# A four-layer graph network on one core: weights loaded later, and the first eight row blocks fed in two halves

## The chip, the cores and the metric

The kernel runs on one core of a Trainium2 chip. The metric is the device time of one execution in microseconds. The kernel before took 1255.84 us in the median of three runs (1253.23 to 1257.3).

## The reference

`x` is 4096 rows of 128 numbers, `adj` a sparse 4096 x 4096 matrix of which about one element in a thousand is not zero. Four layers follow one another; each takes the layer-normalised rows, clipped at zero, and adds its result to x:

```python
h = relu(layernorm(x)); x = x + L0(h, adj)   # relu((D^-1 A' h) W^T + b), A' = a*A + (1-a)*I
h = relu(layernorm(x)); x = x + L1(h, adj)   # two attention heads over the mask adj > 0
h = relu(layernorm(x)); x = x + L2(h, adj)   # one attention head over the mask, relu
h = relu(layernorm(x)); x = L3(h, adj)       # (A^T h) / column sums
```

All is float32. For this change only the start of layer 0 matters: the rows are normalised, multiplied by W (the kernel projects first and sums over neighbours afterwards), and the first products with tiles of `adj` begin.

## The kernel before

**Tiling.** The 4096 rows are 32 blocks of 128 (T = 32). Four groups of eight blocks (Q = 4 groups, S = 8) hold them: X in SBUF, the projected rows in G. The output is made in four quarters of 1024 rows. For a quarter q of a layer, TensorE runs through the 32 blocks k of the sum (`run`, L409): a tile of 128 x 1024 numbers of the transposed `adj` is the stationary operand in eight pieces, the 129 columns of G's block k stream, and the eight results are summed in PSUM (`acc`, L340). A float32 product shows as two MATMUL records, so a tile of eight products counts as 16; a float32 transpose is one record. Five such passes (`h` = 0 to 4) of four quarters make up the kernel.

**The start.** TensorE runs WARM = 38 transposes of the identity, then waits for W0 (`w0_loaded`). A group p is *fed* in four steps. VectorE takes bn_stats of its eight blocks in two halves and derives scale and shift (`statistics`, L847; `scales`, L867). ScalarE normalises X into V (L536). TensorE turns V into `turn` (eight transposes, L355); ScalarE copies `turn` to U in two copies of 512 columns (`widen`, L560); TensorE multiplies U with W0 into `mix` (L374); ScalarE copies `mix` into G in three copies (L612). For group 0 the normalising is divided: ScalarE does blocks 0 to 3 and signals `f_norm`, VectorE does blocks 4 to 7 (L1033 to L1037) and signals `rest_normal`. All eight are turned together, behind both signals.

**The order on each engine.** TensorE's order is written out by hand: `run` takes a dictionary of hooks, a hook of k is executed behind tile k. Each engine executes in its own order, and waits on semaphores. In quarter 0 of layer 0 the groups 1, 2 and 3 are turned and projected as hooks; tile 0, 8, 16 and 24 each wait for their group to be placed in G (`f_placed`). VectorE makes a mask of every tile (`masks`, L1042, one tensor_scalar of 128 x 1024 each) and has the statistics of groups 1 to 3 as hooks; group 1's begin behind mask 0 with a wait for `x_loaded[1]`, and its scale and shift are made behind mask 2.

**The queues.** SyncE issues, in this order: X's blocks 0 to 3 and 4 to 7 (group 0), W0, tiles 0 and 1, X's group 1, tiles 2 and 3, X's groups 2 and 3, then tiles 4 to 31. For quarter 0, eight slots hold tiles (FIRST = 8); tile 8 and later ones wait for their slot. GpSimd makes the identity and then issues 15 loads of weights (0.55 MB together: W2, both heads' projections, biases, gains, the diagonal; `loads`, L319 to L327). They are used by `scores_behind_projections` on TensorE (hook of tile 28), by `prepare` on VectorE behind mask 31, and by ScalarE ahead of quarter 1. GpSimd issues nothing after them.

Of the kernel before, what the change touches and what calls it, by code (L numbers as in the profile page):

```python
# [30 lines left out]
P = 128  # L31
# [33 lines left out]
def graph_layers(nc, x, adj, adj_t, diag, alpha, w0_t, bias0, ff0, ff0_t, ff1_t, attn, g1, b1, g2, b2,  # L65
                 w2, w2_t, a2, out, inputs1):
    N, D = x.shape
    T = N // P
    Q = 4
    S = T // Q  # L70
# [3 lines left out]
    HEADS = 2  # L74
    BANK = 512
    NB = (S + 2) // 3
    STREAM = 4
    FIRST = 8
    DEEP = 32
# [5 lines left out]
    with ExitStack() as ctx:  # L85
# [3 lines left out]
        def sem(name):  # L89
            return ctx.enter_context(nc.semaphore(name))  # L90
# [4 lines left out]
        G = sb("G", [P, 2, T, DW])  # L95
        ring = sb("ring", [P, 5, QC])
        U = sb("U", [P, S * DW])
        V = sb("V", [P, S, D])
        ident = sb("ident", [P, P])
# [20 lines left out]
        w0T = spare[:, 0:D]  # L120
# [22 lines left out]

        acc = ctx.enter_context(nc.psum_tensor("acc", [P, NB, BANK], F32))
        turn = ctx.enter_context(nc.psum_tensor("turn", [P, 2 * BANK], F32))
        mix = ctx.enter_context(nc.psum_tensor("mix", [P, NB, BANK], F32))
        mixed = mix[:, 0:2, :].rearrange("p b c -> p (b c)")
        mixed3 = mixed.rearrange("p (s d) -> p s d", d=D)
# [17 lines left out]
        x_first, rest_normal = sem("x_first"), sem("rest_normal")  # L166
        x_loaded = [sem(f"x_loaded{q}") for q in range(Q)]
# [8 lines left out]

        f_var, f_dev, f_scale, f_norm = sem("f_var"), sem("f_dev"), sem("f_scale"), sem("f_norm")
        f2_var, f2_dev, f2_scale, f2_in = sem("f2_var"), sem("f2_dev"), sem("f2_scale"), sem("f2_in")
        f_turned, f_wide, f_projected, f_placed = sem("f_turned"), sem("f_wide"), sem("f_projected"), sem("f_placed")

        top_placed, top_spread, bias_made, row_shifted = sem("top_placed"), sem("top_spread"), sem("bias_made"), sem("row_shifted")
# [4 lines left out]
        fall_made, fold_made, fixed_v, fixed_w = sem("fall_made"), sem("fold_made"), sem("fixed_v"), sem("fixed_w")  # L186
        acc_paused = [sem(f"acc_paused{b}") for b in range(NB - 1)]
        acc_scaled = sem("acc_scaled")
# [17 lines left out]
        def fixed(v):  # L206
            return isinstance(v, int)
# [105 lines left out]
        @block.gpsimd  # L313
        def _(pool):
            nc.gpsimd.memset(ident[:, :], 0.0).then_inc(ident_zero, 1)
            pool.wait_ge(ident_zero, 1)
            nc.gpsimd.affine_select(out=ident[:, :], in_=ident[:, :], compare_op=ALU.not_equal, fill=1.0,
                                    base=0, pattern=[[-1, P]], channel_multiplier=1).then_inc(consts_made, 1)
            loads = [(bias0_b, bias0.partition_broadcast(P)), (alphac, alpha.partition_broadcast(P)),  # L319
                     (w2raw, w2_t), (attnc[:, 0:4], attn), (attnc[:, 4:6], a2), (dsub[:, :], diag),  # L320
                     (proj1[:, 0:D], ff0_t[0]), (ff0T1, ff0_t[1])]
            loads += [(ff0raw[h], ff0[h]) for h in range(HEADS)]
            loads += [(c, v.rearrange("(c o) -> c o", o=1)) for c, v in ((g1c, g1), (b1c, b1), (g2c, g2), (b2c, b2))]
            loads += [(ff1T[:, :, :], ff1_t.rearrange("h c o -> c h o"))]
            assert len(loads) == WEIGHTS
            for dst, src in loads:
                pool.dma_start(dst, src).then_inc(weights_loaded, 16)  # L327

# [2 lines left out]
        def _(pe):  # L331
# [26 lines left out]
            def feed(p, weights, wide, spreads, posts):  # L358

                def turned():  # L360
                    pe.wait_ge(f_norm, p + 1)
                    if fixed(p) and p == 0:
                        pe.wait_ge(rest_normal, 1)
                    wait(pe, rows_kept, spreads)
                    turn_v().then_inc(f_turned, 1)

                def project():
                    pe.wait_ge(f_wide, p + 1)
                    if fixed(p) and p == 2 * Q:
                        pe.wait_ge(bias_made, late_top[2])  # L370
                    wait(pe, f_placed, p)
                    wait(pe, post_done, posts)
                    for s in range(S):
                        mm = pe.matmul(mix[:, s // 3, (s % 3) * PW:(s % 3) * PW + wide],  # L374
                                       U[:, s * P:(s + 1) * P], weights, start=True, stop=True,
                                       skip_group_check=True)
                    mm.then_inc(f_projected, 1)
                return turned, project
# [30 lines left out]
            def run(h, q, hooks):  # L409
                n = q + h * Q  # L410
                for k in range(T):
                    if h == 0:
                        pe.wait_ge(*loaded0(q, k))
                        if fixed(q) and q == 0 and k % S == 0:
                            pe.wait_ge(f_placed, k // S + 1)
                        lhs, used = tile0(q, k), slot_used
                    elif h == 4:
                        pe.wait_ge(deep_loaded[k % DEEP], (q * (T // DEEP) + k // DEEP + 1) * 16)
                        if fixed(q) and q == 0 and k % S == 0:
                            pe.wait_ge(f_norm, 4 * Q + k // S + 1)  # L420
                        lhs, used = stream3[:, k % DEEP, :], deep_used
                    else:
                        pe.wait_ge(e_made, (n - Q) * T + k + 1)
                        if fixed(q) and q == 0 and k % S == 0:
                            if h == 2:
                                pe.wait_ge(f_placed, 2 * Q + k // S + 1)
                            else:
                                pe.wait_ge(g_scaled[k // S], fixes[h])
                        lhs, used = E[k % EB], e_used
                        if k == 0 and h != 2 and not (fixed(q) and q == 0):  # L430
                            pe.wait_ge(fixed_v, fixes[h])
                    products(n, k, lhs, G[:, h % 2, k, :], used, fixes[h] if h in fixes and fixed(q) and q == 0 else 0)
                    if k in hooks:
                        hooks[k]()
# [4 lines left out]
                pe.transpose(one, ident[:, :], ident[:, :])  # L439
            pe.wait_ge(w0_loaded, 16)  # L440
            own = [feed(p, w0T, D, 0, 0) for p in range(Q)]
            own[0][0]()
            own[0][1]()

            def scores_behind_projections():
                pe.wait_ge(weights_loaded, 16 * WEIGHTS)
                pe.wait_ge(f_placed, Q)
                for h, raw in enumerate(ff0raw + [w2raw]):
                    mm = pe.matmul(one[:, 2 * h:2 * h + 2], raw, attnc[:, 2 * h:2 * h + 2], start=True, stop=True,
                                   skip_group_check=True)  # L450
                mm.then_inc(qv_summed, 1)
            run(0, 0, {2: own[1][0], 4: own[1][1], 10: own[2][0], 13: own[2][1], 18: own[3][0], 21: own[3][1],
                       28: scores_behind_projections})

            def stage0(q, more={}):
# [69 lines left out]
        def _(act):  # L525
# [8 lines left out]
            def normalise(dst, src, mul, add, func, done, n=S):  # L534
                for s in range(n):
                    ins = act.activation(dst(s), src(s), func, bias=add(s), scale=mul(s))  # L536
                if done is not None:
                    ins.then_inc(done, 1)

            def local(t):  # L540
                return lambda s: t[:, s:s + 1]
# [8 lines left out]
            def widen(got, n, done, scale_=None, bias_=None, halves=None):  # L550
# [9 lines left out]
                        ins = act.copy(dst, src)  # L560
                ins.then_inc(done, 1)

            def feed(h, p, q, between=(), ahead=None):

                def of_x(s):
                    return blocks(X, q, 1, s)[:, 0, :]
                if h == 2:

                    act.wait_ge(rows_kept, 1)
                    def known(i):  # L570
                        return lambda s: blocks(norms[:, i, :], q, 1, s)
                    settle()
                    normalise(of_v, of_x, known(0), known(1), ACT.Relu, f2_in)
                    act.wait_ge(f2_in, q + Q + 1)
                    normalise(of_v, of_v, known(2), known(3), ACT.Identity, f_norm)
                else:
                    deviation(f_var, p - Q + 1 if h > 2 else p + 1, f_dev)
                    act.wait_ge(f_scale, p - Q + 1 if h > 2 else p + 1)
                    settle()
                    if h == 4:  # L580
                        normalise(lambda s: blocks(G[:, 0, :, :], q, 1, s)[:, 0, 0:D], of_x, local(scale), local(shift),
                                  ACT.Relu, f_norm)
                        return
                    normalise(of_v, of_x, local(scale), local(shift), ACT.Relu, f2_in if h == 1 else f_norm,
                              S // 2 if fixed(p) and p == 0 else S)
                    if h == 1:
                        deviation(f2_var, q + 1, f2_dev)
                        act.wait_ge(f2_scale, q + 1)
                        normalise(of_v, of_v, local(scale), local(shift), ACT.Identity, f_norm)
                if ahead is not None:  # L590
                    ahead()
                if h in (1, 2):
# [686 lines left out]
```

## Time and profile before

| | |
|---|---|
| median of three runs | 1255.84 us (1253.23 to 1257.3) |
| the profiled execution, its own time | 1257.09 us |
| its span, first to last instruction | 1255.3 us |
| TensorE busy | 1238.2 us, 99% |
| VectorE, ScalarE, GpSimd busy | 751.2 us (60%), 349.8 us (28%), 9.0 us (1%) |
| mean granted TensorE clock | 0.997 |

The profiled execution takes 1.8 us more than its span, and lies 1.25 us above the median. Busy times are measured from the first to the last instruction. TensorE's clock has two levels here, 1.00 (2.4 GHz) and 0.50 (1.2 GHz).

### The profile page before, as it was taken

To read this page: it belongs to the slowest core of one execution; us is meant where nothing else is said; L and a number is where in the kernel's file an instruction comes from. 1 tells how busy PE (TensorE), PEld (TensorE's weight loads), DVE (VectorE), ACT (ScalarE), POOL (GpSimd) and SP (SyncE) were. 2 spreads that over 40 slices of the span, in tenths; PEclk is the share of its full clock that TensorE was granted. 3 is DMA by queue.
4 is the path that set the end of the run, shared out by engine and by line. 5 is a ranking of instruction groups with operands and counts; after the bars stand their busy time and mean duration, and the time that the engine had idled before them with its cause. 6 is when DMAs were issued, how large, how long until landed. Compare 5 with 4: busy or idle time off the path is not lost.

```text
span 1255.3 us, 26479 instructions
## 1 busy us (share of the span) xinstructions
PE 1238.2 (99%) x10979; PEld 1233.2 (98%) x10979; DVE 751.2 (60%) x1342; ACT 349.8 (28%) x872; POOL 9.0 (1%) x21
## 2 busy tenths in 40 slices
PE   7999999999999999999999999999999999999998
PEld 6999999999999999999999999999999999999998
DVE  4437463678786868687979797879687850000001
ACT  3322222243744343531333234343222120000000
POOL 2000000000000000000000000000000000000000
PEclk8999999999999999999999999999999999999999
DMA  8788886830000000000000000000000059999820
GB/s 271 245 263 297 269 288 207 287 110 2 18 1 18 0 17 0 17 1 19 1 17 0 17 1 18 1 1 2 1 0 0 2 199 408 408 411 403 297 68 18
DMA packets 47249, 144.47 MB, mean 115 GB/s; under 512 B 4784, under 2 KB 13248, under 8 KB 47168
## 3 DMA queue, kind: packets, MB, share of 16 engines
q1 hardware_dynamic: 42976, 139.08, 31.1%
q10 hardware_dynamic: 3696, 3.67, 0.8%
q8 instruction: 61, 1.00, 0.3%
q0 software_dynamic: 496, 0.55, 0.2%
q14 instruction: 20, 0.16, 0.0%
HBM read 139.09 MB, written 4.19 MB: 114 GB/s over the span
## 4 chain that ended last, share of the span: by engine, by line
PE 92%; DVE 4%; DMA 2%; ACT 1%; issue 1%; SPq 0%; DVEq 0%; ACTq 0%
PE acc L340 86%; PE mix L374 2%; DVE ring L1010 2%; PE turn L355 2%; PE mix L391 1%; DMA X<-in_x 1%; PE turn L351 1%; ACT V L536 0%; DMA ring<-in_adj_t 0%; DVE stats L851 0%; DVE stats L855 0%; ACT U L536 0%; DVE U L1122 0%; DVE mask L1154 0%; DVE mask L1048 0%
## 5 line engine op out<-in xcount | busy, mean ns | idle before, releaser
L340 PE MATMUL acc<-G,ring 128*128 128x129 f32 x6656 | 758.1, 275 | 2.3 <-DVE ring L1010 1.7
L340 PEld LDWEIGHTS acc<-G,ring 128*128 128x128 f32 x6656 | 750.2, 192 | 5.6 <-DVE ring L1010 3.9
L1010 DVE SCALAR_TENSOR_TENSOR ring<-ring,score,mask 128x1024 f32<-128x1024 f32 x384 | 483.7, 1281 | 136.7 <-PE acc L340 130.6
L340 PE MATMUL acc<-G,mask 128*128 128x129 f32 x3584 | 404.3, 276 | 1.3 <-ACT G L612 1.3
L340 PEld LDWEIGHTS acc<-G,mask 128*128 128x128 f32 x3584 | 403.2, 193 | 1.5 <-issue 1.5
L712 ACT COPY U<-acc 128x387 f32<-128x387 f32 (+1 forms) x60 | 25.5, 459 | 270.6 <-PE acc L340 269.3
L1048 DVE TENSOR_SCALAR mask<-mask 128x1024 f32 (+1 forms) x96 | 64.5, 691 | 58.2 <-DMA mask<-in_adj_t 57.5
L1224 DVE TENSOR_SCALAR zero<-U 128x8 f32<-128x8 f32 x3 | 0.5, 171 | 153.4 <-ACT U L712 153.4
L548 ACT ACTIVATE dev<-var 128x8 f32<-128x8 f32 x28 | 5.9, 210 | 250.7 <-DVE var L864 250.7
L677 ACT COPY ring<-turn 128x512 f32<-128x512 f32 x14 | 8.2, 586 | 121.5 <-DVE ring L1010 114.1
L1048 DVE TENSOR_SCALAR mask<-ring 128x1024 uint8<-128x1024 f32 x32 | 21.9, 693 | 31.4 <-DMA ring<-in_adj_t 21.5
L558 ACT ACTIVATE U<-turn,cols 128x512 f32<-128x512 f32 x32 | 23.2, 774 | 49.4 <-PE turn L355 49.4
L536 ACT ACTIVATE V<-X,shift,scale 128x128 f32<-128x128 f32 (+1 forms) x92 | 36.7, 481 | 0.0
L532 ACT ACT_TABLE_LOAD x26 | 33.4, 1283 | 1.2 <-PEq L1258 0.8
L374 PE MATMUL mix<-ring,U 128*128 128x128 f32 (+2 forms) x256 | 31.4, 276 | 1.2 <-ACT U L560 1.2
L355 PE MATMUL turn<-ident,V 128*128 128x128 f32 x192 | 25.9, 279 | 6.3 <-ACT V L536 4.6
L528 ACT COPY cols<-ident 128x1 f32<-128x1 f32 x44 | 8.6, 195 | 82.4 <-DVE shift L874 34.5
L374 PEld LDWEIGHTS mix<-ring,U 128*128 128x128 f32 x256 | 29.9, 191 | 1.4 <-ACT U L560 1.4
L1243 DVE SCALAR_TENSOR_TENSOR zero<-U 128x3 f32<-128x3 f32 (+1 forms) x3 | 0.5, 162 | 50.8 <-ACT U L712 50.8
L355 PEld LDWEIGHTS turn<-ident,V 128*128 128x128 f32 x192 | 22.3, 144 | 7.0 <-ACT V L536 5.0
L536 ACT ACTIVATE V<-U,shift,scale 128x128 f32<-128x128 f32 x64 | 25.5, 481 | 10.3 <-DVE shift L874 10.3
L612 ACT COPY G<-mix 128x384 f32<-128x384 f32 (+3 forms) x36 | 14.8, 461 | 42.2 <-PE mix L374 42.2
(139 smaller groups left out, 483.4 us busy)
## 6 DMA issues: line engine op xcount, KB each, us to landing
mask<-in_adj SPq DMA_DIRECT2D x128, 512.0 KB, 14.9
mask<-in_adj_t SPq DMA_DIRECT2D x96, 512.0 KB, 4.6
ring<-in_adj_t SPq DMA_DIRECT2D x32, 512.0 KB, 4.6
inputs<-V ACTq DMA_DIRECT2D x4, 512.0 KB, 2.6
V<-inputs SPq DMA_DIRECT2D x4, 512.0 KB, 3.9
X<-in_x SPq DMA_DIRECT2D x3, 512.0 KB, 12.8
out_x<-V ACTq DMA_DIRECT2D x3, 512.0 KB, 14.6
X<-in_x SPq DMA_DIRECT2D x2, 256.0 KB, 2.9
```

Of the source, the lines that this page charges most:

```text
L340: mm = pe.matmul(acc[:, b, (s % 3) * DW:(s % 3) * DW + DW], lhs[:, s * P:(s + 1) * P], g, start=(k == 0 and s % 3 == 0), stop=(k == T - 1) ...
L351: return pe.transpose(dst, col.broadcast_to([P, P]), ident[:, :])
L355: mm = pe.transpose(turn[:, s * P:(s + 1) * P], V[:, s, :], ident[:, :])
L374: mm = pe.matmul(mix[:, s // 3, (s % 3) * PW:(s % 3) * PW + wide], U[:, s * P:(s + 1) * P], weights, start=True, stop=True, skip_group_che ...
L391: mm = pe.matmul(mixed[:, s * P:(s + 1) * P], U[:, s * P:(s + 1) * P], ff1T[:, h, :], start=True, stop=True, skip_group_check=True)
L532: act.activation(warm[func], ident[:, 0:1], func)
L536: ins = act.activation(dst(s), src(s), func, bias=add(s), scale=mul(s))
L558: ins = act.activation(dst, src, ACT.Identity, bias=bias_, scale=scale_)
L612: ins = act.copy(blocks(G[:, h % 2, :, :], q, c, 3 * b)[:, :, 0:D], got[:, :, 0:D])
L712: act.copy(U[:, b * 3 * DW:b * 3 * DW + w], acc[:, b, 0:w]).then_inc(acc_taken, 1)
L1010: dve.scalar_tensor_tensor(E[k % EB], R, rank[h][:, k:k + 1], span(mask, (q * T + k) * QC, QC), ALU.max, ALU.mult).then_inc(e_made, 1)
L1048: dve.tensor_scalar(span(mask, (q * T + k) * QC, QC), tile0(q, k), 0.0, None, ALU.is_gt).then_inc(mask_made, 1)
```

## The change

GpSimd waits for X's group 1 (`x_loaded[1]`) before it issues its 15 loads. Group 0 is turned, widened, projected and placed in two halves of four blocks. The first half has signals of its own (`h_turned`, `h_wide`, `h_projected`, `h_placed`), the second takes those of the group. The first half is turned behind `f_norm`, the second behind `rest_normal`; W0 is still awaited ahead of both. Tile 0 waits for the first half, tile 4 for the second. ScalarE's part of it stands in a function of its own; it places each half with one copy of 4 x 128 columns from `mixed3`, a view of `mix` in which the eight blocks lie 128 columns apart. Group 1 is turned behind tile 4 instead of 2 and projected behind tile 6 instead of 4.

```diff
+    HALF = S // 2
@@ GpSimd
+            pool.wait_ge(x_loaded[1], 16)
             for dst, src in loads:
                 pool.dma_start(dst, src).then_inc(weights_loaded, 16)
@@ TensorE, turned() in feed
-                    if fixed(p) and p == 0:
-                        pe.wait_ge(rest_normal, 1)
@@ TensorE, run
-                        if fixed(q) and q == 0 and k % S == 0:
+                        if fixed(q) and q == 0 and k < S:
+                            if k % HALF == 0:
+                                pe.wait_ge(f_placed if k else h_placed, 1)
+                        elif fixed(q) and q == 0 and k % S == 0:
                             pe.wait_ge(f_placed, k // S + 1)
@@ TensorE, the start
-            own[0][0]()
-            own[0][1]()
+            for half in range(2):
+                pe.wait_ge(rest_normal if half else f_norm, 1)
+                for s in range(half * HALF, (half + 1) * HALF):
+                    mm = pe.transpose(turn[:, s * P:(s + 1) * P], V[:, s, :], ident[:, :])
+                mm.then_inc(f_turned if half else h_turned, 1)
+            for half in range(2):
+                pe.wait_ge(f_wide if half else h_wide, 1)
+                for s in range(half * HALF, (half + 1) * HALF):
+                    mm = pe.matmul(mixed[:, s * P:(s + 1) * P], U[:, s * P:(s + 1) * P], w0T,
+                                   start=True, stop=True, skip_group_check=True)
+                mm.then_inc(f_projected if half else h_projected, 1)
-            run(0, 0, {2: own[1][0], 4: own[1][1], 10: own[2][0], 13: own[2][1], 18: own[3][0], 21: own[3][1],
+            run(0, 0, {4: own[1][0], 6: own[1][1], 10: own[2][0], 13: own[2][1], 18: own[3][0], 21: own[3][1],
@@ ScalarE, instead of widen and the copies into G for group 0
+            def first_halves():
+                for half in range(2):
+                    act.wait_ge(f_turned if half else h_turned, 1)
+                    act.copy(U[:, half * BANK:(half + 1) * BANK], turn[:, half * BANK:(half + 1) * BANK]).then_inc(f_wide if half else h_wide, 1)
+                for half in range(2):
+                    act.wait_ge(f_projected if half else h_projected, 1)
+                    act.copy(G[:, 0, half * HALF:(half + 1) * HALF, 0:D], mixed3[:, half * HALF:(half + 1) * HALF, :])\
+                        .then_inc(f_placed if half else h_placed, 1)
```

## Rows read from the trace of the kernel before

**Rows 1.** The page: span; busy us, share of the span, instructions.

```profile
span 1255.3 us, 26479 instructions
PE 1238.2 (99%) x10979; PEld 1233.2 (98%) x10979; DVE 751.2 (60%) x1342; ACT 349.8 (28%) x872; POOL 9.0 (1%) x21
```

**Rows 2.** TensorE by stage: stretch, length, busy (instructions), granted clock, DMA share, GB/s.

```profile
21.30:24.96 3.66, 0.00 (x0) 0.83 1.00 366
24.96:30.70 5.74, 5.74 (x28) 0.51 0.97 388
...
82.70:1255.30 1172.60, 1164.89 (x10377) 1.00 0.29 105
```

**Rows 3.** TensorE's timeline, 0 to 45 us: start, length, count, idle before it.

```profile
10.08 1.09 PE L355 MATMUL turn<-ident,V 128*128 128x128 f32 x8 [1.71 <-DMA ring<-in_w_t]
12.33 2.05 PE L374 MATMUL mix<-ring,U 128*128 128x128 f32 x16 [1.16 <-ACT U L560]
15.70 5.60 PE L340 MATMUL acc<-G,mask 128*128 128x129 f32 x48 [1.32 <-ACT G L612]
24.96 1.97 PE L355 MATMUL turn<-ident,V 128*128 128x128 f32 x8 [3.66 <-ACT V L536]
26.72 5.58 PE L340 MATMUL acc<-G,mask 128*128 128x129 f32 x32
...
33.92 10.88 PE L340 MATMUL acc<-G,mask 128*128 128x129 f32 x96
44.64 1.04 PE L355 MATMUL turn<-ident,V 128*128 128x128 f32 x8
```

**Rows 4.** Timeline of all engines, 0 to 40 us.

```profile
1.69 0.67 POOL L327 DMA_DIRECT2D ring<-in_bias  x1 [0.21 <-issue]
...
7.15 1.64 ACT L536 ACTIVATE V<-X,shift,scale 128x128 f32<-128x128 f32 x4
...
8.25 0.43 DVE L1037 TENSOR_SCALAR V<-V 128x512 f32<-128x512 f32 x1
...
9.31 0.71 POOL L327 DMA_DIRECT2D ff1T<-in_ff_t  x1
...
11.21 1.07 ACT L560 COPY U<-turn 128x512 f32<-128x512 f32 x2 [2.41 <-PE turn L355]
...
14.42 1.14 ACT L612 COPY G<-mix 128x384 f32<-128x384 f32 x3 [2.14 <-PE mix L374]
...
17.50 0.87 DVE L851 BATCH_NORM_STATS2 stats<-X 128x6 f32<-128x128 f32 x4 [5.14 <-DMA X<-in_x]
...
21.72 3.18 ACT L536 ACTIVATE V<-X,shift,scale 128x128 f32<-128x128 f32 x8
```

**Rows 5.** SP's DMAs issued at 0.75, 1.80, 2.34, 3.29, 16.69: KB, us to landing.

```profile
X<-in_x SPq DMA_DIRECT2D x1, 256.0 KB, 2.8
...
ring<-in_w_t SPq DMA_DIRECT2D x1, 64.0 KB, 8.2
...
mask<-in_adj_t SPq DMA_DIRECT2D x1, 512.0 KB, 9.3
...
X<-in_x SPq DMA_DIRECT2D x1, 512.0 KB, 14.2
...
mask<-in_adj_t SPq DMA_DIRECT2D x1, 512.0 KB, 7.8
```

**Rows 6.** All engines (PE, PEld, DVE, ACT, POOL) by stage, then clock, DMA share, GB/s.

```profile
4.00:9.00 5.00, 4.37 (x28) 4.13 (x26) 4.11 (x21) 1.95 (x6) 5.00 (x10) 1.00 0.51 124
9.00:16.00 7.00, 3.44 (x27) 3.05 (x27) 0.69 (x1) 2.21 (x5) 1.02 (x2) 1.00 1.04 325
16.00:24.00 8.00, 5.30 (x48) 5.11 (x46) 4.56 (x20) 2.58 (x8) 0.00 (x0) 0.98 0.93 304
24.00:30.00 6.00, 5.04 (x24) 5.04 (x25) 4.38 (x14) 1.98 (x5) 0.00 (x0) 0.50 1.00 396
```

**Rows 7.** GpSimd's last load, issued at 9.31: KB, us to landing.

```profile
ff1T<-in_ff_t POOLq DMA_DIRECT2D x1, 128.0 KB, 7.1
```

More of the change, by code:

```diff
@@ L178, in graph_layers @@
         f2_var, f2_dev, f2_scale, f2_in = sem("f2_var"), sem("f2_dev"), sem("f2_scale"), sem("f2_in")
+        h_turned, h_wide, h_projected, h_placed = sem("h_turned"), sem("h_wide"), sem("h_projected"), sem("h_placed")
         f_turned, f_wide, f_projected, f_placed = sem("f_turned"), sem("f_wide"), sem("f_projected"), sem("f_placed")
@@ L589, in feed @@
                         normalise(of_v, of_v, local(scale), local(shift), ACT.Identity, f_norm)
+                if fixed(p) and p == 0:
+                    first_halves()
+                    return
                 if ahead is not None:
```

## The prediction

> **What bounds the kernel now.** I read the page first: TensorE is busy 1238.2 us of a span of 1255.3 [rows 1]. Only 17.1 us of the span are not matmul, and no other engine is near its limit. An edit to the start can therefore pay in two coins alone: idle time of TensorE, and time at the lower clock. The table by stage shows where they lie. From 82.70 us to the end TensorE is idle 7.7 us in 1172.6; at the start it is idle for a whole 3.66 us, and the 5.74 us behind that run at a granted clock of 0.51, that is at 1.2 instead of 2.4 GHz [rows 2]. TensorE's timeline then gives the order of the start [rows 3]: group 0's turn starts at 10.08, 1.71 us behind the warm-up, its projection at 12.33, the first sums at 15.70; after three tiles (48 matmuls, two for each product) TensorE waits until 24.96 for group 1. The brackets there name the releasers: W0's transfer for 1.71 us, ScalarE's normalised V for 3.66 us. The timelines of ScalarE and VectorE [rows 4] follow the second of these back: group 1's normalising starts at 21.72 and takes 3.18 us, its statistics start at 17.50, and they start there because X's second part lands there: it is issued at 3.29 and lands 14.2 us later [rows 5]. W0 is issued at 1.80 and lands 8.2 us later, at 10.0, though X's first 256 KB took 2.8 us [rows 5]. So both waits are DMA waits.
>
> Why is DMA late? From 4 to 9 us the engines move 124 GB/s at a busy share of 0.51, with four SP transfers outstanding; from 9 to 16 us they move 325, and 396 when tiles alone flow [rows 6]. The slow stretch is the one in which GpSimd issues its 15 loads (first at 1.69, last at 9.31) [rows 4]. That the loads cause it is an inference from the coincidence.
>
> **The change, part by part.** I compare with one common point: five tiles summed and group 1 turned. Before, that is at 26.72 + 5.58 = 32.3 us [rows 3].
>
> *Loads behind X's second part.* GpSimd has nothing behind the waiting loads. Their consumers (the scores behind tile 28, the constants on VectorE, ScalarE's second layer) come behind some 70 us; free. Without the loads, 1.64 MB are left to be moved at about 4.2 us (W0, tiles 0 and 1, X's second part). At 325 GB/s these take 5.0 us, so X's second part lands near 9.3 instead of 17.5, W0 near 4.5 (before, 10.0), tile 0 near 6 to 7 instead of 11.6 [rows 5, 6].
>
> *Halves.* W0 no longer holds anything: the turn now waits for the first normalising of V, done at 7.15 + 1.64 = 8.79; VectorE's half is done at 8.68 [rows 4]. TensorE turns from 8.84. One half turned is 1.09/2 = 0.55, to 9.4; ScalarE's copy of 512 columns is 1.07/2 = 0.53, to 9.95; the projection of eight blocks is 2.05 us, from 10.0 to 12.06; the second half's turn (to 9.95) and copy (to 10.5) lie beneath the first half's projection, and the placing of half one (about 0.55) beneath the second's. Sums start at 12.1 instead of 15.70. Placing of half two ends near 12.6 and is wanted at tile 4, near 19.5: hidden. Pieces moved by ScalarE are the same columns; two of 512 replace three of 384, 384 and 256, which is nothing. [rows 3, 4]
>
> *The turn two tiles later.* It runs behind tile 4. A tile is 5.60/3 = 1.87 us, so four tiles reach 12.1 + 7.4 = 19.5; tile 4 and the turn (1.04, as at full clock at 44.64 [rows 3]) would reach 22.4. Is group 1 ready? Its statistics may start at 9.4; before, from their start to the end of normalising went (21.72 + 3.18) - 17.50 = 7.4 us, so it is ready near 17 to 19, ahead of the turn at 21.4. The 3.66 us wait goes. One tile now stands between projection and tile 8; 1.87 us cover ScalarE's placing of 1.14 us. Without that cover the price would be 1.2 us, as at the start.
>
> If no data are late, the gain is 32.3 - 22.4 = 9.9 us; I take 9.8, with 0.1 for waits between halves. It includes the clock: the turn at 1.97 instead of 1.04 and 32 matmuls in 5.58 instead of 3.63 (96 take 10.88) [rows 3] are 2.9 us.
>
> *What is late next: tile 4.* It is wanted at 19.5 and before landed at 16.69 + 7.8 = 24.5 [rows 5]. This is the disputed term. From the landing of X's second part (17.5) to that of tile 4 went 7.0 us, with the same five transfers and no loads between them (the last had landed at 9.31 + 7.1 = 16.4 [rows 4, 7]). Starting from 9.3 this gives 16.3, plus what the loads cost, since they now fall into this stretch. Lower bound: their 0.55 MB at 304 GB/s [rows 6], 1.8 us, tile 4 at 18.1, no wait. Upper bound: all that they seem to have cost before, 17.5 - 9.3 = 8.2 us, tile 4 at 24.5. Between them: the shortfall from 4 to 9 us is 5 x (325 - 124) = 1.0 MB or 3.1 us, with the bytes 4.9. This is a mean over engines while a landing waits for the slowest, so I add 0.5: 5.4 us, tile 4 at 21.7, TensorE idle 2.2 us. Tile 3, wanted at 17.7, would land at 11.9 and with the loads' 5.4 at 17.3. Idle gaps of 1.71, 1.16 and 1.32 us left the clock at 1.00; in the gap of 3.66 it fell [rows 2, 3, 6]. A gap of 2.2 is nearer to the first kind, and I leave the clock up.
>
> What VectorE does bears on that value. In the slow stretch it is busy 4.11 of 5 us, from 9 to 16 us 0.69 of 7, and there the loads flow beside the tiles [rows 6]. In the changed kernel it is busy from 9.4 to about 13.5 with group 1 and three masks, and then only 0.69 us for each tile. The Trainium skill (SBUF — State Buffer, the "DVE blocks DMA" trap) says that GpSimd cannot write its descriptors while a VectorE operation in a two-port mode holds the shared port, and tensor_scalar is one such. By that rule the masks hold up the loads anew and the sum would lie at the upper bound; the trace agrees in that the slow stretch ends with VectorE's work at 8.68, but most of VectorE's work there is statistics, so it does not decide.
>
> Sum: 9.8 - 2.2 = 7.6 us. Against the profiled execution's own 1257.09 this is 1249.5; that execution lies 1.25 above the median of 1255.84, against which I predict 1248.2.
>
> **The rivals.**
>
> *A: the loads move their whole stall.* The bytes up to tile 4 are the same in both kernels and its landing stays at 22.6 to 24.5. For it: the same engines, the same 15 loads. TensorE waits 3.1 to 5.0 us at tile 4 and the clock falls again, worth 2.9. Gain 9.8 - 3.1 - 2.9 = 3.8 down to 1.9: 1252.0 to 1253.9. Chance 0.30.
>
> *B: the loads cost only their bytes.* Tile 4 lands by 19.5 and the gain is 9.8: 1246.0. For it: from 9 to 16 us loads and tiles share 325 GB/s without loss. The Trainium skill (DMA: Bandwidth & Descriptors, Queues, rings and completion order) has each DMA engine go round robin between the queues that have work; by that rule two queues cost each other their bytes and no more. The trace does not agree at 4 to 9 us, where half of the engines' time is unused. Chance 0.14.
>
> *C: the change does not bring W0 forward,* because what is slow from 4 to 9 us is not the loads. Then the turn starts at 10.08, the sums at 13.3, and tile 4 still lands at 24.5, with the lower clock behind it: gain 1.9, 1253.9. Against it: X's first part came through the same queue in 2.8 us just before [rows 5], and later tiles flow at 396 GB/s [rows 6]. Chance 0.08.
>
> *D, on the other side: the masks stretch the loads' stall.* If VectorE's 0.69 us masks double it, tile 4 lands some 5 us later than before, at 29.5. Idle 10.0 and clock 2.9 stand against 9.8: 3.1 us slower, 1258.9. It decides once tile 4 lands past 19.5 + 9.8 - 2.9 = 26.4. Chance 0.05.
>
> **How the numbers follow.** My case (tile 4 at 20.5 to 22.6, gap under 3.1, clock up; gain 6.7 to 8.8, so 1247.0 to 1249.1) has 0.43. A measurement of this kernel can tell about 0.3% (3.8 us) from no change. Faster by more: my case, B, and a part of A in which the clock stays up (0.07), together 0.64. Within: the rest of A, C, and half of D, 0.33. Slower: 0.03. The range runs from B's 1246.0, less 0.5 for the spread of the runs, to A's 1253.9: 1245.5 to 1254.0. My case's own range stands above.
>
> **What would show it.** Right: W0 landing under 5 us and the first turn at 8.8; two waits of under 0.2 us between halves; first sums at 12.1; X's second part landing at 9 to 10; no wait of the turn for V; one wait of 1 to 3 us for tile 4 (5th tile) and a granted clock of 1.00 throughout; behind 30 us the same busy time. Wrong: a first turn still at 10.0 (C); a wait above 3 us at tile 4 with clock 0.50 behind it (A); no wait for data (B); tile 2 or 3 awaited before 17 us, which would mean that the loads stall SP's queue sooner than I have it.

## The result: 1248.57 us against 1256.57

The changed kernel takes 1248.57 us in the median of four runs (1248.33 to 1250.37), the kernel before beside it 1256.57 (1253.23 to 1257.33): ratio 0.9947, with a 95% interval of 0.9935 to 0.9960. (The 1255.84 us that the prediction starts from are the median of the first three runs of the kernel before; a fourth came with the result.) The profiled execution took 1248.47 us, its span is 1246.7, 8.6 us under that of before. In a later comparison on one chip the same kernel, once more, took 1248.34 against 1255.37 (ratio 0.9943, 0.9931 to 0.9955). Medians of several executions are of fast ones; one of the kernel before with the loads' wait, of 1581.82 us at a mean clock of 0.753, was a slow one and is left out.

The page of the changed kernel, as in [rows 1]:

```profile
span 1246.7 us, 26479 instructions
PE 1235.0 (99%) x10979; PEld 1229.9 (99%) x10979; DVE 750.7 (60%) x1342; ACT 349.8 (28%) x871; POOL 9.6 (1%) x21
```

TensorE's busy time fell by 3.2 us although it executes the same 10979 matmuls: most of it is the time at the lower clock (2.9 us by the prediction's sum). The other 5.4 us are idle time. TensorE's timeline of the start, beside [rows 3]:

```profile
8.94 1.06 PE L449 MATMUL turn<-ident,V 128*128 128x128 f32 x8 [1.43 <-ACT V L549]
10.24 2.05 PE L454 MATMUL mix<-ring,U 128*128 128x128 f32 x16 [0.24 <-ACT U L580]
12.17 9.55 PE L343 MATMUL acc<-G,mask 128*128 128x129 f32 x80
21.56 1.04 PE L358 MATMUL turn<-ident,V 128*128 128x128 f32 x8
22.43 3.74 PE L343 MATMUL acc<-G,mask 128*128 128x129 f32 x32
...
34.94 1.04 PE L358 MATMUL turn<-ident,V 128*128 128x128 f32 x8
```

The first turn now waits for ScalarE, not for W0. The wait of 3.66 us is gone. The first sums start at 12.17 instead of 15.70, and the common point of the prediction (five tiles summed, group 1 turned) comes at 21.56 + 1.04 = 22.60 instead of 32.3. Group 2's turn, an event that all kernels here have, starts at 34.94 instead of 44.64. So the start gained 9.7 us.

SP's transfers of W0 (issued at 1.80), X's group 1 (3.28) and tile 4 (9.96), beside [rows 5]; the last column is the time from issue to landing:

```profile
ring<-in_w_t SPq DMA_DIRECT2D x1, 64.0 KB, 3.5
...
X<-in_x SPq DMA_DIRECT2D x1, 512.0 KB, 7.5
...
mask<-in_adj_t SPq DMA_DIRECT2D x1, 512.0 KB, 9.7
```

They land at 5.3, 10.8 and 19.66. Stages of all engines, with the columns of [rows 6]:

```profile
4.00:9.00 5.00, 3.58 (x29) 3.37 (x28) 4.43 (x22) 1.95 (x6) 0.00 (x0) 1.00 0.94 303
9.00:16.00 7.00, 6.76 (x58) 6.49 (x59) 4.79 (x21) 3.53 (x9) 4.93 (x8) 1.00 1.04 322
16.00:24.00 8.00, 7.88 (x71) 7.69 (x70) 2.03 (x3) 3.28 (x8) 4.00 (x8) 1.00 1.03 371
```

From 4 to 9 us DMA moves 303 GB/s where it moved 124, and the loads, now issued from 11.07 to 20.0 us, do not bring the slow stretch with them: 322 and 371 GB/s, with one microsecond at 194 (15 to 16).

Of the 9.7 us, 8.6 are left at the end of this execution. TensorE loses 0.6 at one place, in the last quarter of layer 0, where a tile arrives late for matmuls (VectorE's mask and TensorE wait for the same transfer):

```profile
220.61 0.69 DVE L1074 TENSOR_SCALAR mask<-ring 128x1024 uint8<-128x1024 f32 x1 [2.40 <-DMA ring<-in_adj_t]
...
220.63 3.62 PE L343 MATMUL acc<-G,ring 128*128 128x129 f32 x30 [0.63 <-DMA ring<-in_adj_t]
```

In the same kernel's second profile this wait is absent, and that execution took 1247.61 us. So the change does not bring it in every run.

### The profile page after: what moved, and what is told of

It is laid out like the page before. It is cut to its first block, busy times and chain, and to the rows that moved or that the text cites. A ratio compares the mean times of both kernels' runs of the same rounds, so it can differ in the third digit from the quotient of the medians.

```text
span 1246.7 us, 26479 instructions
## 1 busy us (share of the span) xinstructions
PE 1235.0 (99%) x10979; PEld 1229.9 (99%) x10979; DVE 750.7 (60%) x1342; ACT 349.8 (28%) x871; POOL 9.6 (1%) x21
## 4 chain that ended last, share of the span: by engine, by line
PE 92%; DVE 4%; DMA 2%; ACT 1%; SPq 1%; issue 1%; DVEq 0%; ACTq 0%
PE acc L343 86%; PE mix L375 2%; DVE ring L1036 2%; PE turn L358 2%; PE mix L392 1%; PE turn L354 1%; DMA ring<-in_adj_t 1%; DMA mask<-in_adj_t 1%; SPq L249 0%; ACT V L549 0%; DVE stats L881 0%; ACT U L549 0%; DVE stats L877 0%; DVE U L1148 0%; SPq L264 0%
## 5 line engine op out<-in xcount | busy, mean ns | idle before, releaser
L549 ACT ACTIVATE V<-U,shift,scale 128x128 f32<-128x128 f32 x64 | 25.5, 481 | 10.3 <-DVE shift L900 10.3
L549 ACT ACTIVATE V<-X,norms 128x128 f32<-128x128 f32 (+1 forms) x64 | 25.5, 483 | 0.1
```

## The experiments

Unless said otherwise each is the changed kernel with one edit. Those with a ratio were timed five to eleven times beside the kernel before; those called "one run" have one time and one profile. The last column but one is the start of group 2's turn (44.64 before).

| kernel | us | ratio to before, interval | W0 lands | group 2's turn | note |
|---|---|---|---|---|---|
| changed, again | 1248.34 | 0.9943 (0.9931 to 0.9955) | 5.4 | 34.99 | |
| loads do not wait | 1252.73 | 0.9979 (0.9971 to 0.9988) | 10.4 | 42.12 | |
| before + loads' wait | 1250.02 | 0.9961 (0.9948 to 0.9974) | 5.6 | 36.91 | |
| the same, turn at tile 4 | 1249.99 | 0.9959 (0.9946 to 0.9972) | 5.4 | 38.55 | no halves |
| turn at tile 2 | 1248.38 | 0.9944 (0.9931 to 0.9957) | 5.7 | 35.44 | |
| turn at tile 3 | 1247.47 | 0.9935 (0.9924 to 0.9947) | 5.7 | 34.75 | |
| loads wait for X's group 0 | 1250.69 | one run | 5.5 | 37.66 | |
| loads wait for X's group 3 | 1248.39 | one run | 5.4 | 34.91 | |
| no wait, broadcasts last | 1252.09 | one run | 5.8 | 38.44 | |
| no wait, bias plain | 1252.11 | one run | 5.7 | 37.58 | other numbers |
| no wait, alpha plain | 1252.97 | one run | 11.0 | 40.16 | other numbers |
| no wait, both plain | 1249.98 | one run | 7.2 | 37.59 | other numbers |

For single runs the start says more than the time. With the bias plain and with both plain, group 2's turn comes at the same time (37.58 and 37.59), yet the times are 2.1 us apart; from that turn to the end of the span the traces of all kernels here take 1210.5 to 1211.9 us, and 1212.7 with the bias plain.

### Which part earns the gain

**Without the loads' wait.**

```diff
-            pool.wait_ge(x_loaded[1], 16)
```

> The changed kernel without the one line that makes GpSimd's loads wait for X's group 1. Theory L (loads issued in the first 10 us stall the DMA engines): W0 lands again near 10 us, the first turn starts at 10.1, the sums at 13.3, X's group 1 lands near 17.5 and tile 4 near 24.5; TensorE then waits for tiles 2 to 4, about 4 us in all, and the granted clock may fall: 1252 to 1255 us. Rival C (DMA is slow from 4 to 9 us in any case and the gain is that of the halves and hooks): W0 and tile 4 land as in the changed kernel, 5.3 and 19.6 us, and the time is its 1248.6.

Theory L, within 0.7 us in every point: X's group 1 lands at 16.9 and tile 4 at 25.2. TensorE's timeline:

```profile
10.40 1.09 PE L448 MATMUL turn<-ident,V 128*128 128x128 f32 x8 [2.45 <-DMA ring<-in_w_t]
11.73 2.05 PE L453 MATMUL mix<-ring,U 128*128 128x128 f32 x16 [0.24 <-ACT U L579]
13.65 3.81 PE L342 MATMUL acc<-G,mask 128*128 128x129 f32 x32
18.25 2.05 PE L342 MATMUL acc<-G,mask 128*128 128x129 f32 x16 [0.79 <-DMA mask<-in_adj_t]
20.95 2.05 PE L342 MATMUL acc<-G,mask 128*128 128x129 f32 x16 [0.65 <-DMA mask<-in_adj_t]
25.20 2.85 PE L342 MATMUL acc<-G,mask 128*128 128x129 f32 x16 [2.19 <-DMA mask<-in_adj_t]
27.84 1.91 PE L357 MATMUL turn<-ident,V 128*128 128x128 f32 x8
```

Three waits for tiles, 3.6 us together, take the place of the one for V. The last tile of the three takes 2.85 us instead of 2.05 and the turn 1.91 instead of 1.04: the clock falls (the mean granted clock is 0.72 from 24 to 30 us). What stays of the gain is 2.3 us of 7.

**The loads' wait alone, on the kernel before.**

```diff
+            pool.wait_ge(x_loaded[1], 16)
             for dst, src in loads:
```

> The kernel before with that one line added and nothing else. Theory L: W0 lands at 5.3, the turn starts at 8.9, sums at 14.6 (turn 1.1, copy 1.1, projection 2.05, placing 1.15), three tiles to 20.2 where group 1 is ready (18.2), no wait there, clock 1.00: 2.1 to 2.4 us behind the changed kernel, 1250.8. Rival C: no gain beyond 1 us, 1255.6 to 1256.6.

1250.02 in the median of five: 4.9 us (by the ratio) to 5.1 us (by the medians; before had 1255.07 in this comparison) of the 7.0. It is a little less behind the changed kernel than theory L said. **With the turn at tile 4 too, and still no halves:**

```diff
-            run(0, 0, {2: own[1][0], 4: own[1][1], ...
+            run(0, 0, {4: own[1][0], 6: own[1][1], ...
```

> The kernel before with the loads' wait and with group 1's turn and projection at tiles 4 and 6, so without the halves alone. If the halves are worth what they save between the first turn and the first sums (14.6 against 12.17, 2.4 us, less the 0.3 us that TensorE then no longer waits for tile 4): 1250.7. If they are hidden anyway (rival: tile 4's landing sets the pace): within 0.5 us of the changed kernel, 1248.6 to 1249.1.

1249.99, between the two, and nearer to the first by a little. The halves are not hidden. The cleanest pair is the kernel with the wait alone against the changed kernel with its turn at tile 2, for these differ by the halves only and were timed side by side: 1250.02 (five runs, 1248.99 to 1252.2) against 1248.38 (five runs, 1247.43 to 1248.86), 1.6 us. The traces agree: group 2's turn is at 36.91 and 35.44, the first sums are at 14.52 and 12.31. The kernel of this experiment had a profile with a lower clock in the start, which its 38.55 contains; more of that below.

**The turn's place.**

```diff
-            run(0, 0, {4: own[1][0], 6: own[1][1], ...
+            run(0, 0, {2: own[1][0], 4: own[1][1], ...    # turn_at_2
+            run(0, 0, {3: own[1][0], 5: own[1][1], ...    # turn_at_3
```

> The changed kernel with group 1's turn and projection back at tiles 2 and 4. V of group 1 is ready at 18.2 and tile 2 ends at 17.8: TensorE waits 0.4 us there and no longer 0.3 us at tile 4, so 1248.6, no change. Rival (the later turn is what removes the old wait of 3.66 us): a wait of 1 us or more at the turn, 1249.5 to 1252.

> The changed kernel with group 1's turn behind tile 3 and its projection behind tile 5. V is ready at 18.2, tile 3 ends at 19.5, so no wait for V, and tile 4 is wanted only at 20.5 (landed at 19.6): the 0.3 us wait goes. 0.3 us under the changed kernel, not to be told from it; rival (tile 4's landing moves with the turn): a wait stays.

Turned behind tile 2, TensorE waits 0.52 us for V; behind tile 4 it waited 0.3 us ahead of tile 4; behind tile 3 for nothing:

```profile
12.36 7.38 PE L343 MATMUL acc<-G,mask 128*128 128x129 f32 x64
19.58 1.04 PE L358 MATMUL turn<-ident,V 128*128 128x128 f32 x8
20.46 3.74 PE L343 MATMUL acc<-G,mask 128*128 128x129 f32 x32
```

Here tile 4 landed at about 20.0 and was wanted at 20.46. At 1247.47 this is the fastest of all, and its six runs (1247.32 to 1247.97) reach the changed kernel's six (1247.61 to 1249.19) only at the edge; but the intervals against before overlap, so 0.9 us is more than these runs can vouch for; the start accounts for 0.2 of them (34.75 against 34.99). The part of the change that is named for the turn is worth nothing measurable once the loads wait: V is ready at 18.2 whichever hook asks for it.

> The changed kernel once more, unchanged, beside the others on this chip. 1248.0 to 1249.0; in the profile 9.7 us gained at the start as before, and the 0.6 us wait for a tile of the ring in the last quarter of layer 0 (at 220 us) gone if it is chance, there again if it belongs to the change.

1248.34, as expected: group 2's turn at 34.99 is 9.65 us earlier than before, and the wait at 220 us is gone.

### Why the early loads are so dear

**Another time for the loads.**

```diff
-            pool.wait_ge(x_loaded[1], 16)
+            pool.wait_ge(x_loaded[0], 16)    # wait_x0
+            pool.wait_ge(x_loaded[3], 16)    # wait_x3
```

> The changed kernel with the loads waiting for X's group 0 (about 4.4 us) in place of group 1: the first load is issued near 4.5, in the midst of VectorE's statistics of group 0. Theory L1 (what stalls is a load among SP's transfers at any time of the start, as the broadcasts read slowly): the rate falls to about 125 GB/s from 6.5 to 11 us, tile 1 and X's group 1 land 4 to 5 us later than in the changed kernel. Theory L2 (only loads whose first descriptors come before the DMA queues are full stall; here SP's are): 300 GB/s or more throughout, and X's group 1 lands only by the loads' bytes later, near 12.5. Either way the first turn stays at 8.9 (W0 is ahead).

> The changed kernel with the loads waiting for X's last group. They then start near 17 us and no longer take bytes before tile 4: it should land 0.5 to 1.5 us earlier than 19.6, and TensorE's wait of 0.3 us goes: 0.3 us faster, not to be told from no change. If loads at 17 us stall the engines as at 2 us (theory L1), tiles 5 to 8 land 4 to 5 us late and TensorE waits at tile 5 or 6.

Neither theory of the first had it right: X's group 1 lands on time (10.3), and then one dip of about two microseconds follows. TensorE's table by microsecond (last columns: clock, DMA share, GB/s), first loads issued at 4.77:

```profile
9.00:10.00 1.00, 1.00 (x8) 1.00 1.15 267
10.00:11.00 1.00, 0.76 (x7) 1.00 0.51 152
11.00:12.00 1.00, 1.00 (x12) 1.00 0.40 140
12.00:13.00 1.00, 1.00 (x11) 1.00 0.96 370
```

TensorE then waits 2.79 us for tile 4. Loads behind X's group 3 dip as well, 172 GB/s from 21 to 23 us, but there nobody waits for a tile any more. With them out of the way tile 4 is issued at 9.65 and lands 8.3 us later:

```profile
mask<-in_adj_t SPq DMA_DIRECT2D x1, 512.0 KB, 8.3
```

That is 17.95 against 19.66 in the changed kernel, 1.7 us. It would be the loads' 0.55 MB at 322 GB/s, but that match is luck: the last and largest load is issued only at 19.29, and by 19.66 no more than 0.23 MB of loads have moved. The changed kernel's DMA from 11 to 19.66 us (q1 has SP's transfers, q0 GpSimd's; packets, MB, share):

```profile
q1 hardware_dynamic: 2511, 2.63, 93.3%
q0 software_dynamic: 221, 0.23, 8.9%
```

At the 333 GB/s of this stretch these are 0.7 us. Tile 4 was also issued 0.3 us later, before any load was, and the microsecond at 194 GB/s costs some 0.4. In the changed kernel's second profile tile 4 is issued at 10.06, lands 8.5 us later, at 18.6, and TensorE does not wait for it at all. In the six profiles here whose loads wait for X's group 1 it lands at 18.6 to 20.0. So the loads cost tile 4 0.6 to 2.0 us, against a single profile in which they come later.

**The broadcasts last.** Two of the 15 loads read one row, or one number, into all partitions.

```diff
-            pool.wait_ge(x_loaded[1], 16)
+            loads = loads[2:] + loads[:2]
```

> The changed kernel with the loads not waiting, but the two broadcasts (bias and alpha, read from one row into all partitions) issued last instead of first. Theory B (the broadcasts are what reads slowly and holds the engines): from 4 to 9 us 250 GB/s or more, W0 lands by 6, tile 4 near 20 to 21, about 1249. Rival (any first load through GpSimd's queue does it): 120 to 150 GB/s from 4 to 9 us, W0 near 10, as without the wait.

Half right. W0 comes early and the rate from 4 to 9 us is 322 GB/s, though GpSimd issues plain loads all through it, the first at 1.68; so the slow stretch does not belong to the first loads in the queue, nor to early loads as such. But it follows the broadcasts, now issued at 8.89 and 9.50, to where they are:

```profile
13.00:14.00 1.00, 1.00 (x11) 1.00 0.96 286
14.00:15.00 1.00, 1.00 (x11) 1.00 0.73 143
15.00:16.00 1.00, 1.00 (x11) 1.00 0.29 76
16.00:17.00 1.00, 1.00 (x11) 1.00 0.83 242
```

and tiles 3 and 4 come late, with waits of 1.11 and 2.12 us.

**The broadcasts replaced, one and both.** Still with no wait; layer 0 gets other numbers as bias, as alpha, or both.

```diff
-            loads = [(bias0_b, bias0.partition_broadcast(P)), (alphac, alpha.partition_broadcast(P)),
+            loads = [(bias0_b, w2_t), (alphac, g1.rearrange("(c o) -> c o", o=1)),
```

> The changed kernel without the loads' wait, and with the first load, the broadcast of the 512 B bias row into 128 partitions, replaced by a plain load of 64 KB of W2's transpose into the same place (so layer 0 adds other numbers than the bias). Theory B1 (the bias broadcast is what holds the DMA engines): 300 GB/s or more from 4 to 9 us, W0 lands by 6, tile 4 by 20 to 21, no dip below 200 GB/s in any stretch of 1 us. Theory B2 (the 4-byte broadcast of alpha holds them): the dip of 4 to 9 us stays as without the wait (103 GB/s), W0 near 10. Theory Q (the first transfers of GpSimd's queue, whatever they are): the same as B2.

> The same, with the second load alone replaced: alpha's 4-byte broadcast becomes a plain load of 128 numbers of g1 (so alpha has other values in layer 0). Theory B1: the dip stays, 100 to 150 GB/s from 4 to 9 us and W0 near 10. Theory B2: it goes, 300 GB/s, W0 by 6. Theory Q: it stays.

> Both broadcasts replaced by plain loads, the loads not waiting (so the bias and alpha of layer 0 have other values). With the bias alone replaced, 233 GB/s flowed from 4 to 9 us, against 103 with the broadcasts and 303 with the loads waiting. If the rest of the loss is alpha's broadcast: 300 GB/s or more and tile 4 by 21 us. If it belongs to early loads as such: 220 to 250 GB/s again, tile 4 near 22.3, 1252.

The stretch from 4 to 9 us, first with the bias plain, then with alpha plain, then with both:

```profile
4.00:9.00 5.00, 3.28 (x28) 3.04 (x26) 4.38 (x22) 1.86 (x6) 5.00 (x10) 1.00 0.84 233
```

```profile
4.00:9.00 5.00, 3.48 (x28) 3.25 (x26) 4.11 (x21) 1.95 (x6) 5.00 (x10) 1.00 0.50 120
```

```profile
4.00:9.00 5.00, 3.59 (x28) 3.35 (x26) 4.17 (x22) 1.95 (x6) 5.00 (x10) 1.00 0.80 236
```

Alpha's broadcast does not make the slow stretch: without it the stretch stays as it was, with W0 at 11.0 (group 2's turn does come 2.0 us earlier than in the profile without the wait, 40.16 against 42.12, which is not explained). The bias's broadcast is what holds W0 (10.4 and 11.0 with it, 5.7 and 7.2 without) and takes the rate from 233 to about 110. It is not all: with both broadcasts gone 236 GB/s still fall short of 303, and group 2's turn comes at 37.6 instead of 34.94, 2.7 us later than with the loads behind X's group 1. That early plain loads as such cost this is not shown, and the run with the broadcasts last speaks against it: its plain loads began as early and left 322 GB/s. These are single runs, and their first loads differ.

## Why the prediction was right, and where it was not

The time predicted was 1248.2, the one measured 1248.57, with the mechanism in its main lines. But two terms missed, one against the other, so that the time came out right is in part luck, and my likeliest case (tile 4 at 20.5 to 22.6) is not the one that came.

- **Loads behind X's second part: right.** W0 at 5.3 (predicted near 4.5), X's group 1 at 10.8 (9.3, too early by 1.5; that the rate was 303 and not 325 GB/s is 0.4 us of it, the rest stays open), tile 0 near 7.4. That the loads caused the slow stretch was an inference; taking the wait away alone shows it, and the plain bias shows which load does most of it.
- **Halves: right to 0.1 us.** First turn at 8.94 (8.84), projection 10.24 (10.0), first sums 12.17 (12.1), waits between halves 0.24 us. Without the halves 1.6 us are lost.
- **The turn two tiles later: the wait went as said, but not by the move.** V was ready at 18.2. With the turn back at tile 2 TensorE waits half a microsecond.
- **Tile 4: the term that was mis-sized.** I had it land at 21.7, with the loads costing 5.4 us, of which 3.1 were the old shortfall moved along. It landed at 19.66 (18.6 in the second profile) and TensorE waited 0.3 us instead of 2.2 (nothing in the second). Two errors are in this. The landing without the loads was put at 16.3 and is 17.95, mostly because X's second part lands 1.2 to 1.5 us later than I had it (10.5 in that kernel, 10.8 in the changed one); and the loads cost 1.7 us here (0.6 to 2.0 in six profiles), near my lower bound of 1.8, and not 5.4. The gain at the common point was 9.7, not 7.6. This is nearest to rival B (given 0.14; tile 4 by 19.5), except that B's total of 1246.0 was not reached either. What the shortfall did in place of moving: the bias's broadcast, which had starved the tiles for five microseconds, now ran from 14 to 16 us among transfers of X, and only one microsecond there was below 200 GB/s (194, from 15 to 16; 245 in the second profile).
- **The rest of the run.** "The same busy time behind 30 us" held; of the 1.1 us lost there in the profiled execution 0.6 are a late tile that the second profile does not show; the other 0.5 stay open.
- **From the profiled execution to the median: the second miss.** I carried the 1.25 us between them over. But the runs of before spread more (1252.8 to 1258.4, mean clock 0.995 to 0.999) than those of the changed kernel (1247.6 to 1250.4, clock 0.999 to 1.000): how long the lower clock lasts in the old gap probably differs from run to run. This is argued and not shown: only one run of before is traced (mean clock 0.997, 2.9 us lost), and the others' times go with their mean clocks only loosely (1252.8 to 1256.4 us at 0.998 and 0.999, 1254.7 to 1258.4 at 0.995 to 0.997). The new kernel has no such gap, and its profiled execution (1248.47) lies at its median. So 9.7 us at the start of one execution are 7.0 to 8.0 in the median: 2.1 us more at the start than the 7.6 of the sum, 1.1 lost behind it, and the 1.25 that did not carry over, which together come to almost nothing.

**The rivals.** A (the stall moves whole) and C (W0 not earlier) fall with the landings at 19.66 and 5.3. D (VectorE's masks stretch the loads' stall), and with it the Trainium skill's rule (SBUF — State Buffer, the "DVE blocks DMA" trap), does not show here: from 9 to 16 us VectorE was busy 4.79 of 7 us, group 1's statistics and three masks among it, while GpSimd issued, and DMA moved 322 GB/s; the last load landed 6.1 us from its issue, before 7.1. With the broadcasts last it does not show from 4 to 9 us either: VectorE busy 4.43 of 5 us, GpSimd issuing throughout, 322 GB/s. Of the Trainium skill's round robin between queues (DMA: Bandwidth & Descriptors, Queues, rings and completion order) the traces agree for the loads from 11 us on, but for the microsecond at 194 GB/s, and for the plain loads ahead of the late broadcasts; they do not for the bias's broadcast, nor for the two runs that replace it, which move 233 and 236 GB/s where 303 to 329 flow without loads.

**Open.** Why the rate stays at 233 and 236 GB/s with the broadcast replaced though it is 322 with the same plain loads in another order, and why the broadcasts dip the rate for five microseconds there, for two or three among tiles later (140 to 172, and 76 at worst), and for one among X's rows. That tiles suffer more than X's rows do fits the profiles here, but was not tried by itself.

## What to carry to other kernels

When the first microseconds are short of data, read DMA's rate there before its order: a queue that looks merely late may be starved by small loads that nobody needs yet, and one wait on a semaphore can return them. A load that broadcasts one row to all partitions is worth a trace without it, and a time of its own. And when a gap is removed in which the clock falls, compare medians, not one profile with another: the runs with the gap spread over 5.6 us here, those without it over 2.8.

## What the runs showed of the hardware that was not expected

- A 64 KB broadcast of one 512 B row through GpSimd's queue leaves a total of 103 to 124 GB/s over five microseconds, where 233 flow with a plain load of 64 KB in its place. W0, 64 KB and issued 0.1 us behind it, then lands at 10.0 to 11.0 us in three profiles, and at 5.7 without it (7.2 with both broadcasts replaced).
- The clock can fall without any long gap. In the kernel with the loads' wait and the turn at tile 4 but no halves, no gap of TensorE behind the warm-up was above 1.79 us, and yet the projection and the idle time around it ran at a granted clock of 0.67, the two levels mixed (columns as in [rows 2]; the last three rows are the same stretch by microsecond):

```profile
7.22:9.02 1.80, 0.01 (x2) 1.00 1.09 341
9.02:11.24 2.22, 1.06 (x8) 0.97 1.06 394
11.24:16.17 4.93, 3.61 (x17) 0.67 1.04 289
...
11.00:12.00 1.00, 0.76 (x3) 0.56 1.04 379
12.00:13.00 1.00, 1.00 (x7) 0.50 1.14 311
15.00:16.00 1.00, 0.00 (x0) 1.00 0.66 193
```

It fell behind two gaps (1.79 and 1.16 us) with 1.06 us of work between them, and was back up before the third gap (1.32 us) ended; the projection took 3.60 us instead of 2.05. A second of the five runs may have had the same, by its time and mean clock (1251.6 us at 0.999, as the profiled one's 1251.0; the other three 1249.5 to 1250.0 at 1.000). The kernel before had nearly the same gaps, 1.71 and 1.16 us with 1.09 us of work between them, and kept its clock:

```profile
10.08:15.70 5.62, 3.14 (x24) 1.00 1.05 319
```

The prediction judged the clock by the longest single gap; by these rows that is not enough, and what decides between the two cases is not shown.
